# A four-layer graph network on one core: where the second unit's mean is taken, and which unit is gathered first

## What is computed

```python
def spmm(h): return segment_sum(edge_weight[:, None] * h[src], dst, N)
x = x + spmm(spmm(relu(_layernorm(x))))                       # layer 0: two hops
x = x + gcn(relu(_layernorm(x)))                              # layer 1: h @ W, degree norms, self loops
h = relu(_layernorm(x)); agg = segment_sum(h[src], dst, N)
x = x + relu((h + agg) @ W1.T + b1) @ W2.T + b2               # layer 2
h = relu(_layernorm(x))                                       # layer 3: message MLP, sum, update MLP
m = mlp(concat(h[src], h[dst], edge_attr)); agg = segment_sum(m, dst, N)
x = x + mlp(concat(h, agg))
```

## Time and profile before

| | before |
|---|---|
| median of 3 runs | 5991.66 us (5991.39 to 5993.59) |
| span of the profiled execution | 5088.6 us, mean granted TensorE clock 0.759 |
| outside the span, against the median | 903 us |
| PE / PEld busy | 3604.8 us (71%) / 2894.4 us (57%) |
| VectorE busy | 3000.5 us (59%) |
| ScalarE busy | 2008.8 us (39%) |
| GpSimd busy | 3383.3 us (66%) |
| chain that ended last | GpSimd 44%, issue 24%, DMA 11%, PE 8%, VectorE 6% |
| first source stage, first gather to last centring | 2230 to 3043 us |
| second source stage, first gather to last sum | 3092 to 3855 us |

### The profile page before, as it was taken

One profiled execution on the slowest core, in us unless ns is written; L12 is line 12 of the kernel. 1 busy time (PEld: TensorE's weight loads), 2 busy tenths in 40 slices (PEclk: granted clock), 3 DMA queues, 4 the chain that ended last, 5 costly groups with the idle time before them and its releaser, 6 DMA issues.

```text
span 5088.6 us, 70422 instructions
## 1 busy us (share of the span) xinstructions
PE 3604.8 (71%) x18706; PEld 2894.4 (57%) x18706; DVE 3000.5 (59%) x7177; ACT 2008.8 (39%) x5132; POOL 3383.3 (66%) x2949
## 2 busy tenths in 40 slices
PE   2756666666549999956666667878754888888884
PEld 1534444443349999944444445666643776666663
DVE  5534433443335555547767775888865777676671
ACT  1444334434301111124444444555542555455452
POOL 2777777777658888865554442656565577777774
PEclk9767667667655555568787888989886999999996
DMA  4232332332334444423332222444443233232320
GB/s 137 53 55 43 54 54 43 55 54 47 88 45 72 68 72 71 61 32 100 107 96 87 87 97 77 146 143 145 144 150 108 80 99 112 73 110 71 111 73 20
DMA packets 323012, 424.51 MB, mean 83 GB/s; under 512 B 206656, under 2 KB 224550, under 8 KB 322405
## 3 DMA queue, kind: packets, MB, share of 16 engines
q1 hardware_dynamic: 146932, 335.86, 18.9%
q0 software_dynamic: 176000, 87.72, 14.4%
HBM read 245.53 MB, written 212.59 MB: 90 GB/s over the span
## 4 chain that ended last, share of the span: by engine, by line
POOL 44%; issue 24%; DMA 11%; PE 8%; DVE 6%; ACT 2%; POOLq 1%; DVEq 0%; SPq 0%; ACTq 0%
POOL ga L894 24%; POOL out_x L1030 8%; DMA hop<-acc,osl 7%; POOL hop L931 7%; POOL xu L967 4%; PE mm L1070 2%; PE tp L1225 2%; PE tp L1212 2%; DMA xu<-acc,osl 1%; DMA ga<-table,isl 1%; DVE xin L1922 1%; POOL isl L890 1%; DVE wide L2064 1%; PE mm L1089 1%; DMA ga<-xu,isl 1%
## 5 line engine op out<-in xcount | busy, mean ns | idle before, releaser
L894 POOL DMA_INDIRECT ga<-table,isl x784 | 808.6, 1031 | 271.3 <-issue 230.9
L931 POOL DMA_INDIRECT hop<-acc,osl x392 | 635.6, 1621 | 194.7 <-issue 130.7
L967 POOL DMA_INDIRECT xu<-acc,osl x392 | 620.0, 1582 | 142.6 <-issue 102.4
L1160 PE MATMUL tp<-us,wide 128*128 128x64 f32 x1568 | 341.0, 421 | 350.3 <-DVE us L1906 350.3
L1160 PEld LDWEIGHTS tp<-us,wide 128*128 128x128 f32 x1568 | 336.6, 332 | 356.6 <-issue 356.6
L1030 POOL DMA_INDIRECT out_x<-acc,osl x392 | 438.3, 1118 | 133.8 <-issue 114.7
L1212 PE MATMUL tp<-us,wide 128*128 128x64 f32 x1568 | 416.8, 422 | 120.9 <-DVE wide L2064 120.9
L894 POOL DMA_INDIRECT ga<-xu,isl x392 | 404.2, 1031 | 139.0 <-issue 118.0
L894 POOL DMA_INDIRECT ga<-in_x,isl x392 | 392.4, 1001 | 119.8 <-issue 95.7
L1175 PE MATMUL tp<-xw,cc 128*128 128x394 f32 x784 | 398.5, 603 | 96.3 <-ACT found L1493 96.0
L1212 PEld LDWEIGHTS tp<-us,wide 128*128 128x128 f32 x1568 | 380.0, 332 | 125.4 <-issue 96.3
(11 more groups left out here) (368 smaller groups left out, 8694.2 us busy)
## 6 DMA issues: line engine op xcount, KB each, us to landing
wide<-xu SPq DMA_DIRECT2D x84, 448.0 KB, 4.3
zx<-key_rows SPq DMA_DIRECT2D x28, 896.0 KB, 4.5
out_x<-wide SPq DMA_DIRECT2D x56, 448.0 KB
table<-acc SPq DMA_DIRECT2D x56, 448.0 KB, 2.6
xin<-xs SPq DMA_DIRECT2D x56, 448.0 KB
wide<-table SPq DMA_DIRECT2D x56, 448.0 KB, 7.1
xu<-in_x SPq DMA_DIRECT2D x25, 1000.0 KB, 5.5
hop<-zeros SPq DMA_DIRECT2D x1, 12544.0 KB, 35.6
```

Source lines behind the costliest of these rows:

```text
L894: nc.gpsimd.indirect_dma_start(o[:, g, :], None, table, bass.IndirectOffsetOnAxis(idx[:, g:g + 1], 0)).then_inc(s, 16)
L931: nc.gpsimd.indirect_dma_start(hop, bass.IndirectOffsetOnAxis(osl[b][:, g:g + 1], 0), acc[b][:, g, :], None, bounds_check=hop_max, oob_is_ ...
L967: nc.gpsimd.indirect_dma_start(xu, bass.IndirectOffsetOnAxis(osl[b][:, g:g + 1], 0), acc[b][:, g, :], None, bounds_check=all_max, oob_is_e ...
L1160: t = nc.tensor.matmul(o[:, g * D:g * D + D], equal[b][:, c, (g % 2) * P:(g % 2) * P + P], us[b][:, c, :], start=n == 0, stop=n == 1)
```

## The change

Two edits. In VectorE's pass of the first source stage, the mean of unit 1 no longer opens the pass; it stands behind the centring of unit 0. In the second source stage, GpSimd goes through the units in the order 1, 0, in its waits, slot copies and gathers; the count of finished slot copies that it waits for follows the order and not the unit.

```diff
@@ GpSimd, both source stages @@
                 def body(i, first):
-                    for b in B2K:
+                    for n, b in enumerate(B2K if k == 0 else B2K[::-1]):
                         if not first:
 
                             if k == 0:
...
                             else:
                                 after.wait_ge(*f.ga_free.at(i - 1, ("g", b)))
                         slot_copy(isl[b][:, :], index[:, bass.ds(ecol(i, b), G)])
-                        after.wait_ge(s_slot, base + 2 * i + b + 1)
+                        after.wait_ge(s_slot, base + 2 * i + n + 1)
                         gather(ga[b], table, isl[b], f.got[b])
@@ VectorE, one_pass @@
-                if k == 0:
-                    source_mean(own, i, 1)
                 if k == 1:
                     source_sum(own, i, 1)
                 dense_spread(l, "l2", 0)
...
                 dense_add(l, "x3", 0)
                 if k == 0:
                     source_centre(own, i, 0, first)
+                    source_mean(own, i, 1)
                 dense_centre(own, j, 0)
                 dense_spread(l, "l3", 0)
```

## The result

The changed kernel took 5954.9 us (median of 20 runs, 5924.9 to 6016.66), the kernel before beside it 5989.92 us (20 runs, 5957.58 to 6007.16): a ratio of 0.9951, with a 95% interval of 0.9937 to 0.9964. The change made the kernel 0.5% faster, 35 us, where 195 us had been forecast. The median lies outside the range of 5770 to 5858.

What follows compares the result with a forecast made beforehand. No engine was near full; waits between VectorE and GpSimd's gathers in the two source stages were taken as the bound. Gains of 149.8 + 33 + 12 = 194.8 us off 5991.66 gave 5797 us, range 5770 to 5858.

Steps and rivals of the forecast that it cites:

- The ring of the first source stage: Unit 0's centring, both gathers, landing, top of next pass, centring again: turn 58.02 to 47.6 us, gain 135.2 us.
- C to S: First source stage, from unit 0's centring to the pass's last VectorE operation: 32.2 us, plus 1.0 for the moved mean.
- S to C: First source stage, from a pass's last VectorE operation to unit 0's next centring: 25.8 us falls to 14.4.
- Rival (a): TensorE's clock stays low at the top of first-stage passes, 3.8 us more in 14 passes: 5856 us, chance 0.11.
- The first pass: First source stage's opening pass: 31.0 us before the centring falls to 14.4, gain 16.6, with 1.0 given back.
- The second source stage: Gathering unit 1 first removes VectorE's 39.5 us of gather waits, less 6.6 for a product wait: gain 33 us.
- its end: Second source stage's end, bound by GpSimd: 94.5 us to the last landing falls to 84.6; gain 12 us with unit 1's operations.
- The covers: Slack before moved waits cost time: gathers 5 to 6 us, node rows 3.7, second stage's unit 0 about 9.
- the 903 us between them lie outside the span: Gap between profiled span 5088.6 us and timed median 5991.66, taken as untouched, so the whole gain passes through.
- the wait that I priced at 108.1 us: First source stage: VectorE idle before unit 1's mean (line 2166) in 11 turns, until the gathers land.
- (d): No change: all 28 gathers take 1.67 us, first-stage turn 57 us, about 5985 us; chance 0.02.
- (e): Slower: in the second source stage TensorE's granted clock drops, deciding below mean 0.74; about 6250 us, chance 0.02.

Runs made afterwards that it cites:

- b_again: The kernel before, unedited, run again beside the kernel before: 6075.55 us, ratio 1.0003.
- cols_old: The kernel before, with each unit of the first source stage fetched by 14 plain one-column loads instead of 14 gathers: 5847.22 us, ratio 0.9621.
- busy_pool: The kernel before, with one plain load per unit in the first source stage, then 28 GpSimd fills, each waited for: 5839.7 us, ratio 0.9621.
- a_third: The changed kernel, unedited, run against the kernel before on a chip without the hold-up: 4889.88 us, ratio 0.9597.

## Why the prediction was wrong

- **The ring of the first source stage** was right. On a chip without the hold-up the turn went from 58.02 to 47.67 us, forecast 47.6; C to S is 33.18 in the turn shown, forecast 33.2, and S to C 13.70, the best end of 13.7 to 18.2; over the turns it is 14.6 on average (six of 13.7 us, seven of about 15.3), 14.4 taken, as VectorE waits 1.2 us a turn for the product at line 2135. The 13 turns gave 134.5 us of 135.2. Rival (a), the clock that stays low, did not come: it is 0.90 over the stage, and 1.00 from S to C of the turn shown.
- **The first pass** gave 14.0 us of 16.6. Its S to C fell from 31.0 to 13.7 us, 17.3, but its S came 3.3 us later than in the first trace. The first gathers' landing cost 2.31 us behind C, inside the 13 turns above, where 1.0 was set.
- **The second source stage** gave 34.5 us of 33 (51.17 to 47.72 us a turn), its end 122.7 to 110.7, 12.0 of 12: the last gathered sum is 84.2 us behind the third-last pass's first, forecast 84.6. Between the stages 3.0 came where 1.0 was to be lost, in the last stage 1.9. Sum 200.0 us in the spans (5088.6 to 4888.6), forecast 194.8; span 4888.6, forecast 4894. That the two sums lie 5 us apart owes a little to luck, as the differences have both signs.
- **The covers** held there: GpSimd waits 6.3 us a turn for the centring, forecast 7. Its gathers did get longer, 1102 ns on average against 1031, 28 us over the stage or 2 us a turn: the 0 taken was too low, but inside 0 to 5.1, and the cover bore it. The prediction applied the rule of the Trainium skill (SBUF — State Buffer, Who interferes with whom) to all 14 gathers of the second unit, 10.2 us a turn; the trace has a fifth of that. It was the application that was off. In the trace, 101 of the 104 gathers that start beside one of VectorE's 896-element operations on two SBUF tiles (lines 2098, 2122, 2173 and 2195) are long, over 1.2 us, and none of the other 288, which start beside a reduction, an addition from PSUM, a short operation or nothing. In the first trace of before it is 49 of 63, and none of 329. That agrees with the rule.
- **The failed step** is "the 903 us between them lie outside the span. Neither half of the change touches them". They lie inside the span of the executions timed: 1.7 us are outside it. The trace that I read was of an execution without the hold-up (span 5088.6 us; in sets of runs without it the kernel takes 5089 to 5098), and the median beside it of executions with it. That the profiled one ran on another chip or at another time is inferred from these numbers, as its own time isn't given. In the traces with the hold-up the wait that I priced at 108.1 us does not exist, for C to S is 50.0 us on average instead of 32.2 there, and the gathers have landed by then. The gain was not given back later; it was never on the path of these executions. That the indirect transfers of a stage bring the hold-up is shown; how they do it, and why in some sets only, is open.
- **The rivals.** None named this. (d), the change does what it says without effect, had the right size on these chips and the wrong mechanism: gathers of 1.67 us, where they stayed at 1.04 to 1.08. (e) had its point at a mean clock of 0.74 in the second source stage; it was 0.79 after the change, and 0.78 in before repeated, so the change did not bring it down. Of what would make the prediction wrong, "if the span falls by 195 us and the timed runs don't" came closest, though in the timed ones the span didn't fall either.

The sum was good to 5 us for an execution like the one traced, and the time was 158 us off for those that were timed. A gap of 903 us, 15% of the time, was there to be read before any wait was priced, and it called for a range that holds a case in which the trace is of other executions than the times.

## What to carry to other kernels

Before pricing waits from a trace, hold its span against the time of the same execution; where the two are far apart, the trace may be of another regime, and the sum is worth as much as that regime's share of the runs timed. A wait removed in a ring pays only while nothing else in the ring has already filled it. Long runs of back-to-back indirect transfers on GpSimd deserve a look at what the other engines do meanwhile: here one pause in 14 was worth 9% on one chip and cost 5% on another. Of the kernels that leave nothing out, the changed one is the fastest without the hold-up (4889.88 us), and the changed one with pauses is the fastest with it (5468.46). The changed kernel with pauses wasn't run without the hold-up.

## What the runs showed of the hardware

- **The same kernel has two levels of time, up to 19% apart.** Before took 5098, 5097 and 5089 us in three sets of runs on one chip, and 5990, 6074, 6074 and 6069 in four earlier sets, the last three of them on three other chips, with spreads of at most 1% within a set. Chip and time of the set are not separated.
- **At the slower level GpSimd's indirect transfers hold up TensorE**, and with it VectorE and ScalarE: 7.5 to 21 us in each of the first source stage's 13 turns, with blocks of 28 gathers of 38.6 us (b_again). Plain loads with as many packets don't (cols_old), GpSimd's fills don't (busy_pool).
- **TensorE's records don't show it**: the matmuls end at 2702.10, their release comes at 2716.26, and the idle time that follows carries "issue" or "remote". Such an ending, on several engines at once, is how this is recognised in a list of waits.
- **A gather is long when it starts beside a VectorE operation on two SBUF tiles**: 0.94 us otherwise, 1.53 us on average beside one of 896 elements (a_third, 101 of 104 over 1.2 us).
